# Cross-attention and mixture-of-experts kernel: first-key weights first, expert loads later, block lists in parts, the projection bias on GpSimd, turned blocks taken out later

## What is computed

```python
x = x + attention(layernorm(x), ctx, Wq, Wkv, Wproj, bproj)    # softmax(q k^T * 64**-0.5) v, then @ Wproj + bproj
tokens = layernorm(x)
probs = softmax(tokens @ gate_w.T); top2_w, top2_idx = top_k(probs, 2)
expert_out = silu(tokens @ expert_w[e].T + expert_b[e])        # of the two chosen experts
x = x + (sum of expert_out * top2_w) @ combine_w.T
```

## Time and profile before

| | before |
|---|---|
| median of 3 runs | 1642.24 us (1641.49 to 1644.45) |
| the profiled execution: its time, its span | 1642.6 us, 1640.9 us |
| busy share PE, DVE, ACT, POOL | 92%, 77%, 65%, 53% |
| mean granted TensorE clock | 0.975 |

### The profile page before, as it was taken

How to read it: one execution, slowest core, us unless ns; L and a number is a source line. 1 busy time by engine, 2 the same in 40 slices (tenths; PEclk the granted TensorE clock), 3 DMA queues, 4 the chain that set the end, 5 groups by cost and what they waited for, 6 DMA issues and landing times.

```text
span 1640.9 us, 38420 instructions
## 1 busy us (share of the span) xinstructions
PE 1514.8 (92%) x11712; PEld 1453.6 (89%) x11712; DVE 1269.3 (77%) x3152; ACT 1060.3 (65%) x2890; POOL 877.2 (53%) x1182
## 2 busy tenths in 40 slices
PE   2399999999899999999999999999999999999796
PEld 2389999999899999999899999989999898999675
DVE  3388888888788888888877888877787788777666
ACT  3277777676566776777677667757776676766432
POOL 2165666656554555577665555556566455644410
PEclk8699999999999999999999999999999999999989
DMA  4363333333367777544577777557787777977822
GB/s 160 101 199 96 95 96 96 96 97 97 99 198 216 224 217 218 169 120 133 164 231 231 209 221 222 171 142 236 233 234 230 218 210 227 265 204 221 275 62 77
DMA packets 179805, 287.63 MB, mean 175 GB/s; under 512 B 23571, under 2 KB 114580, under 8 KB 179348
## 3 DMA queue, kind: packets, MB, share of 16 engines
q1 hardware_dynamic: 168852, 255.82, 53.9%
q0 software_dynamic: 10752, 29.37, 5.8%
HBM read 156.38 MB, written 61.60 MB: 133 GB/s over the span
## 4 chain that ended last, share of the span: by engine, by line
PE 73%; DVE 12%; issue 6%; ACT 4%; SPq 3%; POOL 1%; DMA 1%; ACTq 0%; DVEq 0%; POOLq 0%
PE gen_ps L564 20%; PE qk_ps L564 16%; PE o_ps L564 10%; PE proj_ps L564 10%; PE s_ps L564 8%; PE pT_ps L605 6%; PE gen_ps L688 1%; PE gen_ps L655 1%; DVE sums L1019 1%; PE gen_ps L663 1%; DVE neg_max L1012 1%; ACT stage L795 1%; DVE pT_s_lo L954 1%; SPq L500 1%; DVE xn L999 1%
## 5 line engine op out<-in xcount | busy, mean ns | idle before, releaser
L821 ACT ACTIVATE stage<-s_ps,neg_max 128x128 f32<-128x128 f32 x1024 | 292.8, 371 | 145.1 <-DVE neg_max L1012 120.6
L1331 POOL CAST o_s_hi<-stage 128x256 fp32r<-128x256 f32 x256 | 102.1, 399 | 479.2 <-ACT stage L795 475.3
L1322 POOL TENSOR_TENSOR stage<-stage,inv_sums 128x512 f32<-128x512 f32 x256 | 266.4, 1041 | 53.4 <-DVE inv_sums L1021 53.3
L564 PE MATMUL s_ps<-k_s,qk_s 128*128 128x256 f32 x1536 | 226.5, 283 | 39.1 <-DMA k_s<-qk_s 39.0
L564 PEld LDWEIGHTS s_ps<-k_s,qk_s 128*128 128x128 f32 x1536 | 201.6, 189 | 39.7 <-DMA k_s<-qk_s 39.7
L795 ACT CAST pT_s_hi<-pT_ps 128x512 fp32r<-128x512 f32 x256 | 150.8, 589 | 116.1 <-PE pT_ps L605 110.6
L1019 DVE TENSOR_REDUCE sums<-stage 128x4 f32<-128x512 f32 x256 | 172.8, 675 | 62.8 <-ACT stage L821 55.3
L1012 DVE TENSOR_REDUCE neg_max<-s_ps 128x4 f32<-128x512 f32 x256 | 174.0, 680 | 38.9 <-PE s_ps L564 38.9
L954 DVE TENSOR_TENSOR pT_s_lo<-pT_ps,pT_s_hi 128x512 fp32r<-128x512 f32 x256 | 171.8, 671 | 38.8 <-ACT pT_s_hi L795 35.7
L954 DVE TENSOR_TENSOR qk_s<-qk_ps,qk_s 128x512 fp32r<-128x512 f32 x256 | 175.6, 686 | 33.0 <-ACT qk_s L795 32.0
L1333 POOL TENSOR_TENSOR o_s_lo<-stage,o_s_hi 128x256 fp32r<-128x256 f32 x256 | 188.4, 736 | 21.0
(11 more groups left out here) (349 smaller groups left out, 4636.7 us busy)
## 6 DMA issues: line engine op xcount, KB each, us to landing
w_block<-expert_table SPq DMA_DIRECT2D x147, 512.0 KB
k_s<-qk_s SPq DMA_DIRECT2D x512, 128.0 KB
stage<-sorted_x SPq DMA_DIRECT2D x147, 128.0 KB
sorted_y<-stage SPq DMA_DIRECT2D x147, 128.0 KB
x_raw<-in_x SPq DMA_DIRECT2D x32, 256.0 KB
c_raw<-in_ctxT SPq DMA_DIRECT2D x32, 256.0 KB
stage<-in_x SPq DMA_DIRECT2D x32, 256.0 KB
x_kept<-x SPq DMA_DIRECT2D x32, 256.0 KB
```

The costliest lines, as they stand in the source:

```text
L564: mm = pe.matmul(out_ap, l, r, start=start and n == 0, stop=stop and n == len(terms) - 1, skip_group_check=skip)
L821: last = act.activation(probs[p % 2][:, k, :], s_ps[:, k * P:(k + 1) * P], ACT.Exp, bias=neg_max[p % 2][:, k:k + 1])
L1322: pool.tensor_tensor(probs[b][:, :, :], probs[b][:, :, :], inv_sums[b][:, :].unsqueeze(2).broadcast_to([P, 4, P]), ALU.mult).then_inc(prob ...
L1331: pool.tensor_copy(hi[:, :, :], o_full).then_inc(o_hi, 1)
```

## The change

1. The weights come in other parts: columns 0 to 255 of wq, wkv and wkv_rest first (`FIRST`), then the values, then the other columns (`REST`), then wproj. `queries_keys(0, 0)` waits for the first parts alone, head pair 2 for all of them. POOL makes the low parts of the two key rests and both parts of wproj.
2. The expert weights are issued in slots -1, 0 and 1, behind the key spreads of these slots, as 128, 112 and 15 rows and the bias row. The experts are split and stored in slots 2 to 9, the combine weights in slot 10.
3. `list_blocks` falls into `rows_end` (u = 7), `count_blocks` (u = 0 of the next pair), `list_blocks` (u = 1) and `list_outputs` (u = 4).
4. The bias product and its DMAs go; POOL adds the bias to `xb` (`add_bias`, at u = 0), and `add_residual` waits for that.
5. ACT does the early drain behind `qk`, DVE behind `qk` and `row_max`.

```diff
         WEIGHTS = [
...
+            (in_wq[:, :, FIRST], raw_wq[:, :, FIRST]),
+            (wkv[0:P, FIRST], stage[:, 1, FIRST]),
+            (wkv_rest[:, FIRST], stage[:, 2, FIRST]),
...
-            (expertT[P:2 * P - 1, :], stage[0:P - 1, 1, :]),
+            (expertT[P:2 * P - 16, :], stage[0:P - 16, 1, :]),
...
             def load_weights(n):
-                if n in OVER:
-                    sp.wait_ge(w_lo_dve, OVER[n])
+                if n >= EXPERTS_FROM:
+                    sp.wait_ge(w_lo_dve, BY_VECTOR)
+                if n > EXPERTS_FROM:
+                    sp.wait_ge(w_lo_pool, KEYS_BY_POOL)
...
+                if s == -1:
+                    load_weights(EXPERTS_FROM)
+                if s == 0:
+                    load_weights(EXPERTS_FROM + 1)
+                    sp.dma_start(stage[P - 16:P - 1, 1, :], expertT[2 * P - 16:2 * P - 1, :]).then_inc(w_in[EXPERTS_FROM + 1], 16)
...
+                if s == 1:
+                    load_weights(EXPERTS_FROM + 2)
+                if 2 <= s < E - RING + 2:
+                    load_last(s - 2 + RING)
+                if 2 <= s < E + 2:
+                    keep_expert(s - 2)
...
                 if j == 0 and p == 0:
-                    pe.wait_ge(w_hi, FOR_KEYS)
-                    pe.wait_ge(w_lo_dve, FOR_KEYS)
+                    pe.wait_ge(w_hi, FOR_FIRST)
+                    pe.wait_ge(w_lo_dve, FOR_FIRST)
+                if j == 0 and p == 2:
+                    pe.wait_ge(w_hi, PROJECTION)
+                    pe.wait_ge(w_lo_dve, BY_VECTOR)
+                    pe.wait_ge(w_lo_pool, KEYS_BY_POOL)
...
-                    if p == HEAD_PAIRS - 1:
-                        terms.append((ones_s[:, :], pbias[:, :]))
...
@@ scalar engine, each slot @@
-                general(s, "early")
                 if u < 5 and now:
                     qk(i, u + AHEAD)
                 if u >= 5 and nxt:
                     qk(i + 1, u - 5)
+                general(s, "early")
...
@@ vector engine, each slot @@
-                general(s, "early")
...
                 if u == 7 and nxt:
                     row_max(i + 1, 0)
+                general(s, "early")
...
+                if i - 1 in plan.ends:
+                    if u == 0:
+                        count_blocks()
+                    if u == 1:
+                        list_blocks(plan.ends.index(i - 1))
+                    if u == 4:
+                        list_outputs(plan.ends.index(i - 1))
...
@@ GpSimd @@
+            def add_bias(j):
+                pool.wait_ge(xres_in, (j + 1) * 16)
+                if j == 0:
+                    pool.wait_ge(bias_in, 16)
+                pool.tensor_tensor(xb, xb, bias_row[:, :].unsqueeze(1).broadcast_to([P, 2, C]), ALU.add).then_inc(biased, 1)
+            def split_projection():
+                pool.wait_ge(w_in[PROJECTION], 16)
+                raw, hi, _ = SPLIT[PROJECTION]
+                pool.tensor_copy(hi, raw).then_inc(wproj_hi, 1)
+                weight_lo(PROJECTION)
...
                 if i == -1 and u == 4:
...
+                    for n in range(BY_VECTOR, PROJECTION):
+                        weight_lo(n)
+                    split_projection()
+                if 2 <= s < E + 2:
+                    weight_lo(EXPERTS_FROM + s - 2)
```

More of the change, by code:

```diff
@@ L296, in xattn_moe_kernel @@
         gen_ps = [stack.enter_context(nc.psum_tensor(f"gen_ps{b}", [P, 512], F32)) for b in range(BANKS)]
-        x_in, c_in, xres_in, gate_in, bias_in, ebias_in = (
-            sem(n) for n in ("x_in", "c_in", "xres_in", "gate_in", "bias_in", "ebias_in"))
-        w_in = [sem(f"w_in{n}") for n in range(9)]
+        x_in, c_in, xres_in, gate_in, bias_in, biased = (
+            sem(n) for n in ("x_in", "c_in", "xres_in", "gate_in", "bias_in", "biased"))
+        w_in = [sem(f"w_in{n}") for n in range(12)]
         table_stored = [sem(f"table_stored{r}") for r in range(RING)]
@@ L491, in _ @@
             load_ctx(0)
-            for n in range(5):
+            for n in range(EXPERTS_FROM):
                 load_weights(n)
[L494 to L502, removed]
+                if n == FOR_VALUES:
+                    sp.dma_start(gate_raw[:, :, :], gateT.rearrange("(a p) e -> p a e", p=P)).then_inc(gate_in, 16)
+                    sp.dma_start(gate_last[:, :], gateT[C - 1:C, :].broadcast_to([P, E])).then_inc(gate_in, 16)
+            sp.dma_start(bias_row[:, :], bproj.rearrange("(o c) -> o c", o=1).broadcast_to([P, C])).then_inc(bias_in, 16)
             load_ctx(1)
@@ L521, in _ @@
                     load_ctx(i + 2)
[L522 to L527, removed]
+                if s == -1:
[3 more added lines that the diff above has]
+                    sp.dma_start(stage[P - 16:P - 1, 1, :], expertT[2 * P - 16:2 * P - 1, :]).then_inc(w_in[EXPERTS_FROM + 1], 16)
+                    sp.dma_start(stage[P - 1:P, 1, :], expert_b.rearrange("(o n) -> o n", o=1)).then_inc(
+                        w_in[EXPERTS_FROM + 1], 16)
+                    for e in range(RING):
+                        load_last(e)
+                if s == 1:
[4 more added lines that the diff above has]
+                    keep_expert(s - 2)
                 if i == 1 and u == 0:
@@ L928, in _ @@
                 if i == -1 and u == 3:
-                    weight_hi(0)
+                    for n in range(FOR_FIRST):
+                        weight_hi(n)
                 general(s, "mid")
@@ L933, in _ @@
                 if i == -1 and u == 4:
[L934 removed]
+                    for n in range(FOR_FIRST, FOR_VALUES):
                         weight_hi(n)
                 if i == -1 and u == 5:
[L937 to L941 removed]
+                    for n in range(FOR_VALUES, PROJECTION):
+                        weight_hi(n)
+                if 2 <= s < E + 2:
+                    weight_hi(EXPERTS_FROM + s - 2)
                 if i == 0 and u == 1:
@@ L944, in _ @@
                     act.copy(wgate[:, :, 0:E], gate_raw[:, :, :]).then_inc(gate_w_ready, 1)
-                if i == 1 and u == 0:
+                if i == 1 and u == 2:
                     weight_hi(COMBINE_SPLIT)
@@ L1210, in general @@
                         if n + 1 in plan.ends:
-                            list_blocks(plan.ends.index(n + 1), n)
+                            rows_end(plan.ends.index(n + 1), n)
             for e in range(REGIONS):
@@ L1254, in _ @@
                     row_max(i + 1, 0)
+                general(s, "early")
                 if i == -1 and u == 3:
-                    weight_lo(0)
+                    for n in range(FOR_FIRST):
+                        weight_lo(n)
                 general(s, "mid")
@@ L1283, in _ @@
                 if i == -1 and u == 4:
-                    for n in range(1, BY_VECTOR):
+                    for n in range(FOR_FIRST, FOR_VALUES):
                         weight_lo(n)
+                if i == -1 and u == 5:
+                    weight_lo(FOR_VALUES)
                 if i == 0 and u == 0:
@@ L1396, in _ @@
                     split_ctx_lo(i + 1)
+                if u == 0 and before:
+                    add_bias(i - 1)
                 if i == -1 and u == 4:
-                    pool.wait_ge(ebias_hi, 1)
-                    pool.tensor_tensor(bias_s[1], bias_raw, bias_s[0].bitcast(F32), ALU.subtract).then_inc(ebias_lo, 1)
-                    weight_lo(BY_VECTOR)
-                if i == 0:
-                    weight_lo(EXPERTS_FROM + u)
-                if i == 1 and u == 0:
+                    for n in range(BY_VECTOR, PROJECTION):
+                        weight_lo(n)
+                    split_projection()
+                if 2 <= s < E + 2:
+                    weight_lo(EXPERTS_FROM + s - 2)
+                if i == 1 and u == 2:
                     weight_lo(COMBINE_SPLIT)
```

97 lines of the change are left out of this document (45 added, 52 removed).

## The result

The changed kernel takes 1575.24 us (median of 4 runs, 1573.30 to 1578.16), the kernel before 1642.93 us (median of 4, 1641.49 to 1644.45). The ratio is 0.9589, 95% interval 0.9571 to 0.9608: some 67 us less. The forecast was 1563 with a range of 1547 to 1587.

A forecast was written before the change was run, and what follows sets the result against it. PE, busy 92% of the span, was taken as the bound: only less PE work or shorter PE waits gain. 40 - 1 + 21 + 6 + 12 + 1 = 79 us off 1642.6 gave 1563 us, range 1547 to 1587.

The forecast's parts named there:

- The start: Up to the first turn_probs: it comes at 31.4 instead of 71.88 us; 40 us less, bounds 33 and 44.
- Experts moved: Slots 8 and 9: the experts' split on POOL meets normalisation and the bias add; 1 us more.
- Block list: Behind the five block lists: pieces mostly hidden in DVE's idle time end PE's waits and half clock; 21 us less, bounds 10 and 24.
- Bias: All pairs: 64 bias products fewer on PE, add_bias hidden in POOL's idle time; 6 us less, bounds 3 and 7.4.
- Late drain: Where blocks and mixing overlap: expert_out ahead of xbT_lo ends PE's 23 waits for an expert's drain; 12 us less, bounds 6 and 16.
- Tail: In the tail: the same swap of 0.4 us applies to some four waits; 1 us less, bounds 0 and 3.
- keys late: Rival, start: key spreads queue behind expert columns, or a one-engine transfer blocks SP again; 1575 to 1580 us; 8%.
- a share of 0.06: Sign, start: a DMA share meaning one engine of sixteen; no such stretch if the forecast is right.
- The slower one (bank held): Rival, next turned block on PE: the late-drained block holds the bank; 1710 us at 1 us for each of 147 blocks; 2%.
- POOL against DVE: Rival: POOL's add_bias and extra start work hold off DVE where it is on PE's path; up to 41 us, half gives 1584; 5%.
- My condition for it: In the POOL against DVE rival: POOL's instructions hold off those DVE instructions that read two operands from SBUF.

The follow-up runs named there:

- experiment 1: Kernel before with only the second expert transfer of 127 rows cut into 112 and 15 rows, in their old places: 1603.29 us, ratio 0.9787.
- experiment 2: Changed kernel with 127 expert rows in one transfer again, in place of 112 and 15: 1608.16 us, ratio 0.9817.
- experiment 8: Changed kernel with clearing the dump rows and splitting the combine weights moved from pairs 0 and 1 into pair 2: 1573.72 us, ratio 0.9571.
- experiment 3: Kernel before with only the late drain of turned blocks, behind qk on ACT and behind qk and row_max on DVE: 1631.61 us, ratio 0.9947.
- experiment 6: Changed kernel with the bias product moved to slot 5 of its own pair, only in the five pairs a block list follows: 1563.82 us, ratio 0.9522.
- experiment 4: Changed kernel with the late drain of turned blocks undone: 1587.22 us, ratio 0.9657.

## Why the prediction was right, and where not

The time, 1575, is in the range and 12 us above the forecast. The forecast's steps, one by one, with what the marks and experiments gave. No run took back the block list's split or the bias change by itself, so for these two the size rests on marks alone.

- **The start, 40 forecast, 40.5 measured.** First `turn_probs` at 31.41 us, forecast 31.4. That this fits to a tenth is luck: single steps were off and cancelled, the first low part on POOL with 2.65 and not 1.7 us, the cast of wproj with 1.89 and not up to 3.2. The cause is not luck: experiments 1 and 2 show it from both sides.
- **Experts moved, 1 forecast, 5.1 measured.** Only the experts' split in slots 8 and 9 was counted. The step missed what else falls into pairs 0 and 1: clearing the dump rows on SP and splitting the combine weights, 1.6 to 2.9 us (experiment 8). For the rest there are new waits of PE, 1.05 us for keys at 38.74 and 0.86 at 53.77, whose cause was not tested. The `minus_last` instructions that run long beside POOL (up to 1.52 us in place of 0.42) don't explain it, since before they ran as long (up to 1.54) in pairs 0 and 1 as well. When pairs run at full pace from the start, one-off work that used to lie in a lull no longer does.
- **Block list, 21 forecast, about 13.5 measured** (16.1 of the five pairs, less 1.1 for the bias and 1.5 for the late drain, which is what these pairs gain in experiment 3; as they gain as much in experiment 1, which leaves the drain alone, the figure may be off by 1 to 2 us). This is the largest term that was mis-sized, and the reason is a cost that I had put on another account: `add_bias` was costed at nothing because POOL is idle enough. POOL is (though the instruction takes 1.31 us and not 1.04), but DVE instructions are held beside it. The forecast wanted idle times under 1 us behind the lists; they are 1.27 to 2.11. Without the hold the term is about 23 (13.5 and 9.5 of experiment 6), near the forecast.
- **Bias, 6 forecast, about 7 measured**: 0.21 us in a plain pair and 0.25 to 0.30 in most fuller ones, times 31.
- **Late drain, 12 forecast, 9 to 11 measured** (8.7 alone, 11 when undone, 8.7 as what is left of the marks when list and bias are taken off).
- **Tail, 1 forecast, 4.7 measured**, which says nothing of the swap, since the tail varies by more than that from kernel to kernel, and the granted clock with it.

Sum of what was measured (with 8.7 for the late drain): 40.5 - 5.1 + 13.5 + 7 + 8.7 + 4.7 = 69.3 us, the difference of the spans. It closes because the 8.7 is a remainder; the test of the late drain is experiments 3 and 4. Against the forecast's sum the list and the moved experts lost some 12 us and the late drain 1 to 3; that the total is only 10 short owes 4 us to the tail, which is luck.

**Of the rivals**, keys late came true only in part: PE waits 1.05 us for keys at 38.74. The 1.99 us at 82.11 hang on the one-off works of experiment 8, not on the expert loads, and there is no stretch at a share of 0.06. The slower one (bank held) did not come at all. POOL against DVE came true in part: 9 to 11 us at the five lists, while the 27 other bias products cost nothing that the ratios show, though five of them held `top_w` for 1.60 us. It had been priced as half of all POOL time added, 21 us, at 5%; it should have stood in the sum, with the price read where list and bias product meet, since both had been put in slot 0. My condition for it, DVE instructions with two operands from SBUF, was too narrow too: `tensor_scalar` with one such operand (L1172, L1173) was held up to 2.04 us. The Trainium skill (SBUF — State Buffer, "SBUF: two separate sides") speaks of an exclusive lock for a whole instruction between DVE and GpSimd, and the trace agrees as far as the end of the hold, which comes with the end of POOL's instruction; the start of the hold, up to 0.8 us before that instruction began, is more than this says.

## What to carry to other kernels

Look at the slowest dimension of a transfer before anything else: 127 rows against 112 and 15 made 35 to 37 of the 67 us, by one line. When work goes to an idle POOL, ask not only whether POOL has room but what DVE does in the same microseconds; move it away from chains of short DVE instructions that PE waits for. And when a long stall at the start is removed, list the one-off work that lay beside it, for it now meets the steady loop.

## What the runs showed of the hardware

- A 128x9 instruction of 0.17 us on DVE (`tensor_tensor` or `tensor_scalar`) took up to 2.14 us beside POOL, and a 128x4 `scalar_tensor_tensor` of 0.16 us took 1.60; a `tensor_reduce` of 0.69 us beside the same bias product kept its time. The hold began while POOL's scatter ran, up to 0.8 us before the bias product started, and ended with it. Beside a scatter with nothing ready behind it the same instruction took 0.17 us (experiment 6), and with the order turned round the hold was 1.21 us at most. That the waiting POOL instruction keeps DVE out before it starts would fit all three; what happens inside is left open.
- An 8 KB issue on SP took 16.64 us (16.34 in experiment 2) behind a transfer of 127 rows, 0.25 us behind 112 and 15 rows.
- POOL casts 128x2048 to fp32r in 1.89 us and needs 4.57 us for the subtraction of the same size.
- In the tail, where PE is busy for 38 to 39 us in 50, the granted clock of the same stretch was 0.86, 0.90 or 0.97 from kernel to kernel, with 163.6, 158.5 and 153.9 us for the tail. Why it falls in one and not in the other was not settled.
